# Router stage rebuilt as a pipeline over its eight turns

## The reference, cut to what matters

```python
h = _layernorm(x, axis=-1) * (1 + cb) + sb
x = x + gb * _L0_ffn_ref(h, ...)
# in _L0_ffn_ref:
xn = x_flat * jax.lax.rsqrt(jnp.mean(x_flat * x_flat, axis=-1, keepdims=True) + EPS) * norm_weight
logits = xn @ router_w.T + router_b
probs = jax.nn.softmax(logits, axis=-1)
gates, idx = jax.lax.top_k(probs.T, cap)
xe = xn[idx]
```

## Time and profile before

| | us |
|---|---|
| median of three runs | 3559.85 |
| lowest and highest | 3551.4, 3559.95 |
| the profiled execution, from its first to its last instruction | 3562.3 |
| PE busy in it | 3068.6 |
| DVE busy | 2811.6 |
| ACT busy | 2413.7 |
| POOL busy | 619.7 |

### The profile page before, as it was taken

One profiled execution on the slowest core, in us unless ns is written; L12 is line 12 of the kernel. 1 busy time (PEld: TensorE's weight loads), 2 busy tenths in 40 slices (PEclk: granted clock), 3 DMA queues, 4 the chain that ended last, 5 costly groups with the idle time before them and its releaser, 6 DMA issues. The chain is left out here.

```text
span 3562.3 us, 52805 instructions
## 1 busy us (share of the span) xinstructions
PE 3068.6 (86%) x14840; PEld 2033.9 (57%) x14840; DVE 2811.6 (79%) x10325; ACT 2413.7 (68%) x4471; POOL 619.7 (17%) x749
## 2 busy tenths in 40 slices
PE   7999996254389999999999999999999999998564
PEld 5777775243256566665656656656665665665333
DVE  5777775572488898988888989889898898987475
ACT  5777774112278788887877878788887888787310
POOL 0000001165201121112111111112111111211222
PEclk9999998577699999999999999999999999998776
DMA  1000000313100000000000000000000000000000
GB/s 51 1 0 0 0 0 1 102 21 52 61 1 1 19 13 2 1 25 7 1 25 7 1 19 13 2 19 11 4 1 25 7 1 1 1 1 1 7 0 24
DMA packets 31565, 46.58 MB, mean 13 GB/s; under 512 B 5264, under 2 KB 21712, under 8 KB 31312
## 3 DMA queue, kind: packets, MB, share of 16 engines
q1 hardware_dynamic: 25680, 39.47, 3.3%
q0 software_dynamic: 5632, 4.20, 0.9%
HBM read 35.17 MB, written 8.49 MB: 12 GB/s over the span
## 5 line engine op out<-in xcount | busy, mean ns | idle before, releaser
L1743 DVE TENSOR_SCALAR t_feat_q<-t_recip,t_neg_mean 128x256 f32<-128x256 f32 x1024 | 393.5, 446 | 137.6 <-ACT t_recip L1599 130.2
L1446 PE MATMUL t_o_ps<-t_feat_q,t_wo 128*128 128x512 f32 x1024 | 477.9, 600 | 13.4 <-issue 10.8
L1591 ACT ACTIVATE t_recip<-t_feat_q,t_z_scale 128x256 f32<-128x256 f32 x1024 | 434.8, 498 | 1.7 <-DVE t_feat_q L1743 1.0
L1577 ACT ACTIVATE t_exp_k<-t_k_ps 128x1024 f32<-128x1024 f32 x256 | 259.7, 1015 | 251.5 <-PE t_k_ps L1423 251.5
L1706 DVE CUSTOM_DVE_ANT_0 t_junk<-t_v_ps,t_feat_k 128x256 f32<-128x256 f32 x1024 | 390.5, 418 | 27.0 <-PE t_v_ps L1423 26.8
L1696 DVE SCALAR_TENSOR_TENSOR t_feat_k<-t_exp_k,t_k_ps 128x256 f32<-128x256 f32 x1024 | 369.0, 416 | 31.2 <-ACT t_exp_k L1577 31.1
L1581 ACT ACTIVATE t_exp_q<-t_q_ps 128x1024 f32<-128x1024 f32 x256 | 261.6, 1022 | 93.4 <-PE t_q_ps L1423 93.1
L1732 DVE SCALAR_TENSOR_TENSOR t_feat_q<-t_exp_q,t_q_ps 128x1024 f32<-128x1024 f32 x256 | 312.6, 1221 | 8.8
L1446 PEld LDWEIGHTS t_o_ps<-t_feat_q,t_wo 128*128 128x128 f32 x1024 | 195.1, 191 | 190.3 <-issue 169.8
L1869 POOL TENSOR_TENSOR t_var_eps<-t_moments,t_ln_eps 128x4 f32<-128x4 f32 x128 | 69.4, 542 | 1272.5 <-DVE t_moments L1754 1272.5
L1421 PE MATMUL t_v_ps<-t_x_hi,t_w_hi 128*128 128x512 f32 x512 | 265.6, 519 | 26.8 <-DVE t_w_lo L1687 17.1
(11 more groups left out here) (354 smaller groups left out, 7276.6 us busy)
## 6 DMA issues: line engine op xcount, KB each, us to landing
t_raw_w<-in_wk SPq DMA_DIRECT2D x8, 512.0 KB, 3.5
t_raw_w<-in_wq SPq DMA_DIRECT2D x8, 512.0 KB, 4.4
t_raw_w<-in_wv SPq DMA_DIRECT2D x8, 512.0 KB, 5.5
t_raw_o<-in_wo SPq DMA_DIRECT2D x8, 512.0 KB, 3.3
t_raw<-in_w SPq DMA_DIRECT2D x16, 256.0 KB, 2.7
x<-in_x SPq DMA_DIRECT2D x4, 512.0 KB, 7.2
tokens_dram<-r_hn SPq DMA_DIRECT2D x8, 256.0 KB, 2.3
e_w_raw<-in_fc_w SPq DMA_DIRECT2D x4, 512.0 KB, 4.0
```

Source lines behind the costliest of these rows:

```text
L1446: last = pe.matmul(o_ps[:], wo[:, chunk, :], feat_q[:, s, chunk, :], start=(chunk == 0), stop=(chunk == NC - 1), skip_group_check=True)
L1577: act.activation(exp_k[:], k_ps[:], ACT.Exp, bias=-1.0).then_inc(c["k_exp"], 1)
L1591: last = act.activation(recip[:, q % 2, k * UNIT + n * SEQ:k * UNIT + (n + 1) * SEQ], feat_q[:, s, chunk, cols], ACT.Ln, bias=1.0, scale=z ...
L1743: last = dve.tensor_scalar(feat_q[:, s, chunk, cols], recip[:, q % 2, k * UNIT + n * SEQ:k * UNIT + (n + 1) * SEQ], -1.0, neg_mean[:, s, n ...
```

## The change

The router's loads go out in attention's block. In `router_phase` the loops are written out, semaphores start at 0, and each engine follows a plan of steps in which several turns are under way. `r_turned_h` gets three buffers (`DEEP`), `r_square` two; `r_mean_sq`, `r_ms_eps`, `r_rms`, `r_scaled` and `r_logits_ps` hold all 32 tiles. `r_scaled` and `route` are formed once, at the end. SyncE's wait for the stores is taken out, and GpSimd waits for them ahead of its first gather. The router's persistent tensors are allocated ahead of attention's.

```diff
             sp.wait_ge(w_in, 48)
+            sp.dma_start(g["router_w"][:], d["router_w"]).then_inc(g["router_in"], 16)
+            sp.dma_start(g["norm_w"][:], d["norm_w"]).then_inc(g["router_in"], 16)
+            sp.dma_start(g["router_b"][:], d["router_b"].partition_broadcast(P)).then_inc(g["router_in"], 16)
...
         @block.sync
         def _(sp):
-            start_counters(sp, [*c.values(), *hn_stored])
-            sp.dma_start(router_w[:], d["router_w"]).then_inc(w_in, 16)
-            sp.dma_start(g["norm_w"][:], d["norm_w"]).then_inc(w_in, 16)
-            sp.dma_start(router_b[:], d["router_b"].partition_broadcast(P)).then_inc(b_in, 16)
...
-            for s in range(2):
-                sp.wait_ge(hn_stored[s], 8 * TURNS + 1)
+            for n in range(TURNS):
+                sp.wait_ge(c["hn_ready"], n + 1)
+                sp.dma_start(g["tokens_dram"][n * GT * P:(n + 1) * GT * P, :].rearrange("(t p) d -> p t d", p=P), hn[:, n % 2, :, :])\
+                  .then_inc(hn_stored[n % 2], 16)
 
         @block.gpsimd
...
+            for k in range(TURNS + 4):
+                if k < TURNS:
+                    rstd_of(k)
+                if k >= 4:
+                    rms_of(k - 4)
 
         @block.scalar
         def _(act):
+            def modulate(n):
+                act.wait_ge(c["x_turned"], n + 1)
+                if n >= 2:
+                    act.wait_ge(c["logits_filled"], n - 1)
...
+            for k in range(TURNS + 1):
+                if k < TURNS:
+                    modulate(k)
+                if k >= 1:
+                    square_up(k - 1)
 
         @block.vector
...
+            def find_moments(n):
+                for t in range(GT * n, GT * n + GT):
+                    dve.bn_stats(stats[:, t, :], g["x"][:, t, :]).then_inc(c["bn_done"], 1)
+                dve.wait_ge(c["bn_done"], GT * n + GT)
+                for t in range(GT * n, GT * n + GT):
+                    dve.bn_aggr(moments[:, t, :], stats[:, t, :]).then_inc(c["stats_ready"], 1)
...
+            def scale_rows(n):
+                dve.wait_ge(c["rms_ready"], n + 1)
+                if n >= 2:
+                    dve.wait_ge(hn_stored[n % 2], 16 * (n // 2))
                 for i in range(GT):
...
+            for k in range(TURNS + 5):
+                if 2 <= k < TURNS + 2:
+                    normalise(k - 2)
+                if k >= 5:
+                    scale_rows(k - 5)
+                if k < TURNS:
+                    find_moments(k)
+            dve.wait_ge(c["logits_filled"], TURNS)
+            dve.tensor_tensor(scaled[:], logits_ps[:], rms[:].broadcast_to([P, TILES, EXPERTS]), ALU.mult).then_inc(c["scaled_ready"], 1)
+            dve.wait_ge(c["scaled_ready"], 1)
+            dve.tensor_tensor(g["route"][:], scaled[:].rearrange("p t e -> p e t"),
+                              router_b[:].unsqueeze(2).broadcast_to([P, EXPERTS, TILES]), ALU.add).then_inc(c["scaled_ready"], 1)
...
         @block.tensor
...
+            def turn_h(n):
+                pe.wait_ge(c["h_ready"], n + 1)
+                if n >= DEEP:
+                    pe.wait_ge(c["hn_ready"], n - DEEP + 1)
+                    pe.wait_ge(c["squared"], n - DEEP + 1)
...
+            for k in range(TURNS + 1):
+                if k < TURNS:
+                    turn_x(k)
+                if k >= 1:
+                    turn_h(k - 1)
...
+            for s in range(2):
+                pool.wait_ge(g["hn_stored"][s], 8 * TILES // 4)
```

More of the change, by code:

```diff
@@ L554, in router_phase @@
         h_t = sb("r_h_t", [P, 2, GT * P])
[L555 to L560, removed]
-        turned_x = [ps(f"r_turned_x{i}", [P, GT * P]) for i in range(2)]
[L562 to L566, removed]
+        square = sb("r_square", [P, 2, GT, D])
+        mean_sq = sb("r_mean_sq", [P, TILES, 1])
+        ms_eps = sb("r_ms_eps", [P, TILES, 1])
+        rms = sb("r_rms", [P, TILES, 1])
+        hn = g["hn"]
+        scaled = sb("r_scaled", [P, TILES, EXPERTS])
+        turned_x = [ps(f"r_turned_x{i}", [P, GT * P]) for i in range(2)]
+        turned_h = [ps(f"r_turned_h{i}", [P, GT, D]) for i in range(DEEP)]
+        logits_ps = ps("r_logits_ps", [P, TILES, EXPERTS])
+        names = ("w_ready bn_done stats_ready var_ready rstd_ready xn_ready x_turned h_ready h_turned logits_filled squared "
+                 "ms_ready rms_ready hn_ready scaled_ready").split()
         c = {n: sem("r_" + n) for n in names}
-        hn_stored = [sem(f"r_hn_stored{s}") for s in range(2)]
+        hn_stored = g["hn_stored"]
         block = ctx.enter_context(nc.Block())
@@ L583, in _, with rstd_of @@
-            for s in range(2):
-                sp.wait_ge(hn_stored[s], 8 * TURNS + 1)
+            for n in range(TURNS):
+                sp.wait_ge(c["hn_ready"], n + 1)
+                sp.dma_start(g["tokens_dram"][n * GT * P:(n + 1) * GT * P, :].rearrange("(t p) d -> p t d", p=P), hn[:, n % 2, :, :])\
+                  .then_inc(hn_stored[n % 2], 16)
         @block.gpsimd
         def _(pool):
[L588 to L594, removed]
+            def rstd_of(n):
+                tiles = slice(GT * n, GT * n + GT)
+                pool.wait_ge(c["stats_ready"], GT * n + GT)
+                pool.tensor_tensor(var_eps[:, tiles].unsqueeze(2), moments[:, tiles, 1:2], g["mod_eps"][:, 0:GT].unsqueeze(2), ALU.add)\
+                    .then_inc(c["var_ready"], 1)
+                pool.wait_ge(c["var_ready"], n + 1)
+                pool.tensor_tensor(rstd[:, tiles], var_eps[:, tiles], g["neghalf"][:, 0:GT], ALU.pow).then_inc(c["rstd_ready"], 1)
@@ new lines, in rms_of @@
+            def rms_of(n):
+                tiles = slice(GT * n, GT * n + GT)
+                pool.wait_ge(c["squared"], n + 1)
+                pool.tensor_tensor(ms_eps[:, tiles, :], mean_sq[:, tiles, :], g["mod_eps"][:, 0:GT].unsqueeze(2), ALU.add).then_inc(c["ms_ready"], 1)
+                pool.wait_ge(c["ms_ready"], n + 1)
+                pool.tensor_tensor(rms[:, tiles, :], ms_eps[:, tiles, :], g["neghalf"][:, 0:GT].unsqueeze(2), ALU.pow).then_inc(c["rms_ready"], 1)
+            for k in range(TURNS + 4):
[3 more added lines that the diff above has]
+                    rms_of(k - 4)
@@ L630, in turn @@
[L630 to L635, removed]
-                for i in range(GT):
[L637 to L647, removed]
+            dve.wait_ge(g["router_in"], 48)
+            dve.tensor_scalar(router_w[:], router_w[:], g["norm_w"][:, 0:1], None, ALU.mult).then_inc(c["w_ready"], 1)
+            def find_moments(n):
[4 more added lines that the diff above has]
+                    dve.bn_aggr(moments[:, t, :], stats[:, t, :]).then_inc(c["stats_ready"], 1)
@@ new lines, in normalise @@
+            def normalise(n):
+                dve.wait_ge(c["rstd_ready"], n + 1)
+                if n >= 2:
+                    dve.wait_ge(c["x_turned"], n - 1)
+                for i in range(GT):
+                    t = GT * n + i
+                    last = dve.tensor_scalar(xn[:, n % 2, i, :], g["x"][:, t, :], moments[:, t, 0:1], rstd[:, t:t + 1],
+                                             ALU.subtract, ALU.mult)
+                last.then_inc(c["xn_ready"], 1)
+            def scale_rows(n):
+                dve.wait_ge(c["rms_ready"], n + 1)
+                if n >= 2:
+                    dve.wait_ge(hn_stored[n % 2], 16 * (n // 2))
+                for i in range(GT):
+                    last = dve.tensor_scalar(hn[:, n % 2, i, :], turned_h[n % DEEP][:, i, :], rms[:, GT * n + i, :], None, ALU.mult)
+                last.then_inc(c["hn_ready"], 1)
@@ L2280, in block0 @@
             setup_phase(nc, sem, d, g)
-            causal_attention_phase(nc, sem, d, g)
             with ExitStack() as ctx:
                 local = lambda n, s, t=F32: ctx.enter_context(nc.sbuf_tensor(n, s, t))
+                g["router_w"] = local("r_w", [P, EXPERTS])
+                g["router_b"] = local("r_b", [P, EXPERTS])
+                g["hn"] = local("r_hn", [P, 2, 4, D])
+                g["router_in"] = sem("r_in")
+                g["hn_stored"] = [sem(f"r_hn_stored{s}") for s in range(2)]
+                causal_attention_phase(nc, sem, d, g)
                 g["route"] = local("route", [P, EXPERTS, TILES])
```

63 lines of the change are left out of this document (20 added, 43 removed).

## The result

| | before | after |
|---|---|---|
| median us | 3559.47 | 3524.71 |
| profiled execution's time | | 3521.41 |
| its span | 3562.3 | 3519.7 |
| router stage in it (end of attention to s_top) | 84.25 | 39.52 |

Both medians are of four executions. One execution of the changed kernel, of 8734.81 us, was disturbed and is outside the ratio, though inside the median 3524.71; the other three are 3509.91, 3521.41 and 3528.01, with 3521.41 as their median.

A forecast was written before the change was run, and what follows sets the result against it. No engine bounds the router stage, a chain through four engines does. Start, iterations and tail put the next phase at 636.0, plus 1.2 for the port 637.2 against 680.29: 43.1 us less, 3559.85 to 3517; range 3505 to 3526.

The forecast's parts named there:

- rival (b): Router middle: VectorE alone is the bound, iterations 5 to 7 take 3.2 us each, time 3510; chance 0.06.
- Start: Boundary from attention to router: loads gone from the stage, VectorE starts 0.65 us after attention's end.
- Pieces: Router operations per turn: find_moments 1.15 us, four r_xn 1.03, four r_hn 1.04, rstd pair 1.275, rms pair 1.29.
- Ring: Router iterations 5 to 7: GpSimd's rstd and rms, then VectorE's r_hn and statistics, in a row, 4.96 us each.
- The shared port: Router iterations 5 to 8: GpSimd operations delayed by VectorE's r_xn, 0.3 us each, 1.2 in all.
- Rival (a): Router: normalise waits for the whole GpSimd power, 1.01 us in four iterations, 4.0 in all, time 3521; chance 0.14.
- Tail: Router's end: from the last r_xn to the last r_hn 8.7 us, then route's two operations 0.9.
- Sum: Whole router stage: next phase starts at 637.2 instead of 680.29, 43.1 us less; span 3519.2, median 3517.
- Rival (c): Router's tail: TensorE's clock rises to 2.4 GHz, matmuls halve, 2.5 us less, time 3514; chance 0.12.
- Rival (d): Behind the router: stores and weight loads meet or gathers wait, 2 to 10 us given back, 3519 to 3527; chance 0.08.
- (e): Eight layers: slower through TensorE's clock, each point worth up to 23 us, 3575 at 0.955; chance 0.01.
- (f): Router: the pipeline does not overlap, a turn still 8 us, only some 20 us saved, time 3540; chance 0.02.

The follow-up runs named there:

- rms_first: Changed kernel with GpSimd's two pairs swapped, rms of turn k-4 ahead of rstd of turn k; stage 36.21 us against 39.52, ratio to before 0.9858.
- warm_only: Changed kernel plus only unused 128x512 TensorE matmuls, four at the start and one behind each turn up to turn 6; stage 40.52 us.
- wide_after_xn: Changed kernel plus one unused 128x1024 VectorE tensor_scalar behind r_xn in steps 5 to 8; step 5.10 us, stage 40.02 us.
- wide_before_xn: Changed kernel plus one unused 128x1024 VectorE tensor_scalar ahead of r_xn in each of four steps; step 5.32 us, stage 40.92 us.
- late_after: Changed kernel with 228 unused bn_stats on VectorE at the start of the router stage; stage 83.58 us, ratio to before 0.9997.
- store_wait_back: Changed kernel with SyncE's wait for the stores back at the end of the router phase; stage 40.81 us.
- warm: Changed kernel with rms ahead of rstd, a shorter tail and unused 128x512 matmuls (ten at the start, one behind each turn's logits up to turn 5); stage 34.73 us.

## Why the prediction came out as it did

The span was forecast at 3519.2 and measured 3519.7; the median at 3517, with 3524.71 and 3511.09 on either side. The mechanism held; two sizes did not, and part of the match is luck. By its time alone 3511.09 would fit rival (b), 3510, as well; the r_hn starts 4.98 apart in that run's profile exclude it.

- *Start.* Boundary 0.65, measured 0.54; first r_xn forecast 3.4 us after attention's end, measured 3.38. Right.
- *Pieces.* Statistics of a turn 1.15, measured 1.19 (596.47 to 597.66); an iteration without r_hn 2.18, measured 2.19. Right.
- *Ring.* 4.96 forecast, 4.98 measured, idle 1.7 forecast and 1.66 measured. rms_first removed it by order alone, warm_only left it untouched at double the clock of TensorE: shown.
- *The shared port.* The step that failed: "I take 0.3 for each of four iterations (5 to 8), 1.2 in all". r_var_eps took 0.21 against 0.20, so the term was nothing. The price was read from a tensor_scalar of 1024 columns, and r_xn has 128; with 1024 columns put there the delay did appear, 0.35 a step. Rival (a) fell with r_xn itself, four rows in 1.08 beside the power, and with 0.69 in wide_after_xn. The Trainium skill's rule ("SBUF — State Buffer", "Who interferes with whom") that the later one waits for the whole instruction fits r_var_eps in wide_before_xn, 0.56; it does not fit the 0.69, nor a power that is late at its end, 1.27.
- *Tail.* From the last r_xn's end (625.61) to route's end (634.75) 9.14, forecast 9.6: TensorE's groups overlap, 3.31 for a sum of 3.9, while route took 1.05 in place of 0.9. The r_hn of turn 5 waited 0.35 us for a store, which I had not foreseen; it cost nothing, as VectorE then stood 2.15 us in front of the next r_hn.
- *Sum.* Stage 41.15 forecast, 39.52 measured. The port's 1.2 and the tail's 0.46 are the difference. The span nevertheless matched because from s_top on the first profile took 2.4 us longer than that of before, 1.9 of it in the top-2 phase, while attention had ended 0.26 sooner. In the fourteen profiles the part from s_top to the end took 2869.8 to 2889.1 us, with before at 2882.0, and the same code of the top-2 phase 189.8 to 198.9 in ten of them. So the match to 0.5 us is luck.
- *Rival (c), the clock.* It stayed at 0.50 (1.2 GHz) although TensorE was busy 5.00 of 5 us twice, and in rms_first in four such windows in a row, 605 to 625. Busy time, from which I had argued by the earlier trace rows, did not tell it. With the 128x512 matmuls in the idle time at the start and in the turns the clock was 1.00; no run has them in one of the two places alone.
- *Rival (d).* late_after at 0.9997 excludes that the changed program gives back or gains more than 0.14% behind the stage. (b), (e) and (f) did not come.

What stays open is why the two sets of one program (3521.41 and 3511.09) lie 38 and 51 us below before, for a stage 44.7 us shorter; the spread behind the stage is large enough for it. The times go with TensorE's mean granted clock: of the first set, 3509.91 had 0.936 and 3528.01 had 0.931. What moves the clock no run shows. In the layers the granted clock was 0.99 in the profile of store_wait_back (span 3507.0) and 0.98 in that of wide_after_xn (span 3525.5), over 2300 us each:

```profile
955.00:3255.00 2300.00, 2186.53 (x8760) 1381.97 (x8761) 2028.39 (x7745) 1855.85 (x2601) 386.68 (x426) 0.99 0.02 8
```

```profile
955.00:3255.00 2300.00, 2190.54 (x8729) 1385.54 (x8730) 2020.62 (x7722) 1851.80 (x2598) 385.56 (x422) 0.98 0.02 8
```

## What to carry to other kernels

When a chain over several engines is turned into a pipeline, look for the ring that its orders make: here two engines in fixed order tied rms of an old turn to the statistics of a new one, and swapping two calls was worth 1.7 us a step and 3.3 in the stage. Put work that is ready ahead of work that waits. When an end is shortened by moving operations into a wait, compare their length with that wait, not with what they cost before.

## What the hardware showed that I had not expected

- TensorE was busy for 5.00 of 5 us, twice in a row (four times in rms_first), with transposes of 128 columns and matmuls of 8, at a granted clock of 0.50. With matmuls of 128x512 in its gaps, from attention's end on, it was granted 1.00 through the same work (warm, 595 to 625).
- A GpSimd power operation beside a VectorE tensor_scalar of 1024 columns ended 0.26 us late (1.27 for 1.01), while the VectorE operation was not held up.
- With tensor_scalars of 128 columns there was next to nothing of it: r_var_eps stayed at 0.21 and the power at 1.01 beside r_xn. One r_ms_eps of the changed kernel, at 625.13 beside the last r_xn, took 0.27 in place of 0.20:

```profile
625.13 0.27 POOL L589 TENSOR_TENSOR r_ms_eps<-r_mean_sq,mod_eps 128x4 f32<-128x4 f32 x1 [0.46 <-ACT r_square L616]
```

- The clock that TensorE was granted in one and the same phase differed from profile to profile, 0.67 to 0.72, and the phase's length with it, 198.9 to 189.8 us.
